# A mixture-of-experts layer on one core: tokens 1024 to 2047 routed through their eight experts alone, sorted by expert with indirect transfers

## What is computed

```
probs = sigmoid(x @ router_w.T + expert_bias)          # x: 2048 x 128, 160 experts
top_w, top_idx = top_k(probs, 8)
top_w = top_w / (sum(top_w) + 1e-9) * 2.5
combine = zeros(T, 160); combine[t, top_idx[t]] = top_w[t]
h1 = silu(einsum('th,eih->eti', x, w_gate))            # 64 inner columns an expert
routed = einsum('eti,ehi->th', h1 * combine.T[:, :, None], w_down)
shared = silu(x @ w_gate_shared.T) @ w_down_shared.T
out = x1 + gate_b * (routed + shared)
```

## Time and profile before

| what | us |
|---|---|
| median of three runs | 525.28 (525.02 to 528.24) |
| the profiled execution, whole | 521.39 |
| its span, from the first to the last instruction | 519.6 |
| PE busy | 495.6 (95%) |
| DVE busy | 431.3 (83%) |
| ACT busy | 392.2 (75%) |
| POOL busy | 150.6 (29%) |

### The profile page before, as it was taken

How to read it: one execution, slowest core, us unless ns; L and a number is a source line. 1 busy time by engine, 2 the same in 40 slices (tenths; PEclk the granted TensorE clock), 3 DMA queues, 4 the chain that set the end, 5 groups by cost and what they waited for, 6 DMA issues and landing times.

```text
span 519.6 us, 7819 instructions
## 1 busy us (share of the span) xinstructions
PE 495.6 (95%) x2159; PEld 396.0 (76%) x2159; DVE 431.3 (83%) x513; ACT 392.2 (75%) x440; POOL 150.6 (29%) x144
## 2 busy tenths in 40 slices
PE   7686699999999999999999999999999999999996
PEld 5475488777787788888888788788888888888885
DVE  5999888787878788787888797887878888788886
ACT  3267687787878787888888787878878787878873
POOL 3787434222222222222222222222222222222210
PEclk9699899999999999999999999999999999999999
DMA  7000899999999999999999999999999999999962
GB/s 240 1 1 8 216 226 265 227 225 226 234 227 233 242 236 240 230 235 239 230 239 231 221 241 233 232 245 234 237 236 239 242 239 244 233 239 231 225 176 81
DMA packets 38934, 110.15 MB, mean 212 GB/s; under 512 B 6564, under 2 KB 10788, under 8 KB 38920
## 3 DMA queue, kind: packets, MB, share of 16 engines
q1 hardware_dynamic: 38596, 109.32, 88.5%
q10 hardware_dynamic: 324, 0.67, 0.4%
HBM read 107.58 MB, written 2.38 MB: 212 GB/s over the span
## 4 chain that ended last, share of the span: by engine, by line
PE 74%; DMA 13%; DVE 8%; SPq 2%; issue 1%; ACT 1%; POOL 0%; DVEq 0%
PE ps L921 37%; PE ps L906 37%; DMA cb<-combine_scratch 10%; DVE gu L722 2%; DMA combine_scratch<-combT_b 1%; DMA x_sb<-x 1%; DVE stT L686 1%; SPq L280 1%; DVE picked L715 1%; DVE bn L600 1%; DVE picked L703 0%; PE ps L860 0%; DVE mod_gate L659 0%; DVE xn L615 0%; DVE top L698 0%
## 5 line engine op out<-in xcount | busy, mean ns | idle before, releaser
L722 DVE TENSOR_TENSOR gu<-ps,cb 128x1024 f32<-128x1024 f32 x161 | 196.7, 1222 | 76.8 <-DMA cb<-combine_scratch 69.3
L509 ACT ACTIVATE ps<-ps 128x1024 f32<-128x1024 f32 x161 | 162.1, 1008 | 62.8 <-PE ps L906 60.1
L729 DVE TENSOR_TENSOR g_lo<-gu,g_hi 128x1024 fp32r<-128x1024 f32 x162 | 199.8, 1233 | 0.1
L522 ACT ACTIVATE g_hi<-gu 128x1024 fp32r<-128x1024 f32 x162 | 170.9, 1055 | 29.2 <-DVE gu L722 24.7
L404 POOL TENSOR_TENSOR w_lo<-w_raw,w_hi 128x384 fp32r<-128x384 f32 x98 | 99.7, 1017 | 312.1 <-DVE g_lo L729 312.1
L906 PE MATMUL ps<-h_hi,w_hi 128*128 128x512 f32 x324 | 103.8, 401 | 4.1 <-DVE gu L722 1.7
L906 PE MATMUL ps<-h_hi,w_lo 128*128 128x512 f32 x324 | 102.1, 396 | 0.0
L906 PE MATMUL ps<-h_lo,w_hi 128*128 128x512 f32 x324 | 102.1, 396 | 0.0
L921 PE MATMUL ps<-g_lo,w_hi 128*128 128x512 f32 x324 | 100.6, 392 | 1.5 <-DVE g_lo L729 1.5
L921 PE MATMUL ps<-g_hi,w_hi 128*128 128x512 f32 x324 | 101.1, 393 | 0.0
L921 PE MATMUL ps<-g_hi,w_lo 128*128 128x512 f32 x324 | 101.0, 392 | 0.0
(11 more groups left out here) (99 smaller groups left out, 206.9 us busy)
## 6 DMA issues: line engine op xcount, KB each, us to landing
cb<-combine_scratch SPq DMA_DIRECT2D x322, 256.0 KB, 5.1
w_raw<-experts SPq DMA_DIRECT2D x54, 384.0 KB, 7.0
x_sb<-x SPq DMA_DIRECT2D x4, 256.0 KB, 4.9
out<-xn SPq DMA_DIRECT2D x3, 256.0 KB, 2.2
combine_scratch<-combT_a ACTq DMA_DIRECT2D x1, 512.0 KB, 5.5
wmod_sb<-wmod SPq DMA_DIRECT2D x1, 384.0 KB, 3.5
combine_scratch<-combT_a SPq DMA_DIRECT2D x1, 384.0 KB, 3.1
proj_sb<-proj SPq DMA_DIRECT2D x1, 272.0 KB, 4.9
```

Source lines behind the costliest of these rows:

```text
L509: act.activation(slot(z), slot(z), ACT.Silu).then_inc(silu_done, 1)
L522: act.activation(g_hi[:, k % RING, :], gu[:, k % RING, :], ACT.Copy).then_inc(hi_ready, 1)
L722: dve.tensor_tensor(gu[:, k % RING, :].rearrange("p (b n) -> p b n", b=2), slot(z), cb[:, k % RING, :].rearrange("p (b n) -> p b n", b=2), ...
L729: dve.tensor_tensor(g_lo[:, k % RING, :], gu[:, k % RING, :], g_hi[:, k % RING, :].bitcast(F32), ALU.subtract).then_inc(lo_ready, 1)
```

## The change

Tokens 0 to 1023 keep the dense way: 81 pair steps. They are cut in two pieces: pairs 0 to 44 (`DRAIN_TURN = 4`), and pairs 45 to 80 after the middle stage. For tokens 1024 to 2047 the following is new.

1. **Ranks (in the prologue).** DVE marks the chosen experts (`mark`), PE counts them with eight matmuls of 160 columns and ranks each token among those of its expert with 60 more (`count`, `rank`), DVE makes offsets and, for each token, the eight rows of the sorted order that it goes to (`place`, `row_idx`). `select`, `combine_weights` and `turn_combine` of these tokens go.
2. **Send (beside pairs 0 to 44).** POOL issues 64 indirect transfers (8 tiles x 8 choices), each of which scatters 128 rows of 512 bytes from `xn` to `x_rows` in DRAM: 6 and 6, then 5 behind each `weights_lo`.
3. **Middle stage, dense work stands still.** The shared expert for these tokens (2 block groups); 16 loads of 256 KB of sorted rows, turned on PE, kept by ACT and DVE (`load_sorted`, `turn_x`, `keep_x`); then 56 block groups of four blocks of 128 rows: 40 groups with the first 128 slots of each of the 160 experts, and 16 with 64 extra blocks for experts that have more, whose expert is read from a table at run time. A group is four plain float32 matmuls 64x128 (`block_inner`), one `silu` of ACT, four float32 matmuls 128x128 (`block_down`) and four copies of DVE that wait for each other (`keep_y`), with places read from memory into registers (`TENSOR_LOAD`) on PE and on DVE. Last, 16 banks are turned back and stored (`turn_y`, `keep_turned`, `y_rows`).
4. **Fetch (beside pairs 45 to 80).** POOL issues 64 indirect gathers from `y_rows`: from the third `weights_lo` on, 6 ahead of each, and 16 at the end. DVE adds each with its weight (`add_back`): 32 between the pairs, 32 after the last pair.

```diff
+ST = TILES - DT
+SLOTS = ST * P * TOPK
+BLK = 4
+FULL = NE // BLK
+EXTRA = 64
+XIN, WSR, WOV = 4, 2, 8
...
+            def load_full_weights(group):
+                slot = group % WSR
+                if group >= WSR:
+                    free = (WG * 2 * (group - WSR + 1) - 1 - SHARED) // BLK
+                    sp.wait_ge(yg_done, SH_GROUPS + free + 1)
+                sp.dma_start(ws_g[:, slot, :], experts[group, :, 0:WG * P]).then_inc(ws_loaded[slot], 16)
+                for a in range(2):
+                    sp.dma_start(ws_d[:, slot, a, :], experts[group, a * INTER:(a + 1) * INTER, WG * P:2 * WG * P]
+                                 ).then_inc(ws_loaded[slot], 16)
...
+            def load_extra_gates(first, end):
+                for o in range(first, end, BLK):
+                    if o >= WOV:
+                        sp.wait_ge(yg_done, extra_group(o - WOV) + 1)
+                    _, at = nc.values_load_multi_w_load_instructions(
                        tab_i[1:2, o:o + BLK], engines=(SP_ENGINE,), min_val=0,
                        max_val=WGROUPS * P * 12 - 12 * P + 11, skip_runtime_bounds_check_because=BOUNDED)
+                    for b in range(BLK):
+                        sp.dma_start(w_extra((o + b) % WOV)[0], gate_rows[bass.ds(at[b], P, 12), :]
+                                     ).then_inc(wov_gate[(o + b) % WOV], 16)
...
+            def block_inner(n):
...
+                if n >= 2:
+                    pe.wait_ge(g_done, n - 1)
...
+                for b in range(BLK):
...
+                        pr, a = full_expert(m, b)
+                        if b == 0 or pr % WG == 0 and a == 0:
+                            pe.wait_ge(ws_loaded[pr // WG % WSR], 48 * (pr // WG // WSR + 1))
...
+            for n in range(SH_GROUPS, ZGROUPS):
+                if n + 1 < ZGROUPS:
+                    block_inner(n + 1)
+                if n + 1 == TABLE:
+                    turn_table()
+                block_down(n)
...
+            for i in range(1, DRAIN_TURN + 1):
+                for s in range(BODY // WG):
+                    weights_lo(WG * i + s + 2, (s + 2) % RING)
+                    more = min(sent + 5, ST * TOPK)
+                    send(sent, more)
+                    sent = more
...
+            for n in range(back, ST * TOPK):
+                add_back(n)
```

More of the change, by code:

```diff
@@ L73 @@
 assert PAIRS == TURNS * BODY and WGROUPS * WG == PAIRS
+assert A_GU + RING * CHUNK == 2 * COLS
+PE_ENGINE, DVE_ENGINE = mybir.EngineType.PE, mybir.EngineType.DVE
+SP_ENGINE, POOL_ENGINE = mybir.EngineType.SP, mybir.EngineType.Pool
+BOUNDED = "the table is computed from counts that sum to the number of slots"
 def adaln_layer(nc: bass.Bass, x: bass.AP, columns: bass.AP, log_dt: bass.AP, rows: bass.AP,
@@ L305, in turn @@
                         sp.wait_ge(w_split, group + 1)
[L306 to L308 removed]
+                        load_weights(group + RING, k // WG)
+                    if not ((last or drain) and k + RING >= BODY):
                         sp.wait_ge(gated, j + 1)
                         load_combine(j + RING, k % RING)
[L312 to L318, removed]
@@ L770, in _, with pair @@
-            for c in range(CHUNKS):
-                if c > 0:
-                    turn(c, 0, False)
-                with dve.Fori(1, TURNS - 1) as i:
-                    turn(c, i, False)
-                turn(c, TURNS - 1, True)
+                    pair(i, k, (last or drain) and k == BODY - 1)
+            def pair(i, k, stop):
+                j = BODY * i + k
+                if not stop:
+                    ahead = k + 1
+                    use = BODY // RING * i + ahead // RING + 1
+                    dve.wait_ge(cb_loaded[ahead % RING], 32 * (use - (ahead % RING == 0)))
+                    gate(j + 1, ahead % RING, ahead)
+                gated_lo(j, k)
@@ new lines, in _ @@
+            first = BODY * (DRAIN_TURN + 1)
+            dve.wait_ge(cb_loaded[0], 32 * (first // RING))
+            gate(first, 0, 0)
+            back = 0
+            for i in range(DRAIN_TURN + 1, TURNS):
+                for k in range(BODY):
+                    pair(i, k, i == TURNS - 1 and k == BODY - 1)
+                    at = BODY * (i - DRAIN_TURN - 1) + k - 16
+                    if at >= 0 and at % 5 < 4:
+                        add_back(back)
+                        add_back(back + 1)
+                        back += 2
+                        if back == TOPK * GT:
+                            finish_sparse(0)
@@ L1016, in _, with turn @@
-            for c in range(1, CHUNKS):
-                turn_ffn(c, c)
+                    pe.wait_ge(w_split, WG * i + ahead // WG + 1)
+                inner(ahead % RING, ahead)
+            def turn(i, last, drain):
+                for k in range(BODY):
+                    next_inner(i, k, last or drain)
+                    down(BODY * i + k, k, last and k == BODY - 1)
+            with pe.Fori(1, DRAIN_TURN) as i:
+                turn(i, False, False)
+            turn(DRAIN_TURN, False, True)
```

809 lines of the change are left out of this document (642 added, 167 removed).

## The result

| | before | after |
|---|---|---|
| median (range) | 525.15 us (524.75 to 528.24, 4 runs) | 758.71 us (757.64 to 760.62, 4 runs) |
| span of the profiled execution | 519.6 us | 756.6 us |

The changed kernel takes 1.443 times as long (95% interval 1.437 to 1.450). The forecast was 688 us in a range of 590 to 790: right in sign and inside the range, 71 us too low.

A forecast was written before the change was run, and what follows sets the result against it. The prediction took PE and the DMA transfers to be both full. Its terms, 205 + 23 + 305 + 20 + 112 + 17, gave a span of 682 us and a median of about 688, in a range of 590 to 790 us.

The forecast's parts named there:

- pair 44 ends: End of the first dense part: 189 us, plus 4 for routing and 12 for the send, 205 us.
- 56 block groups: Middle stage: 332 us at half clock, 249 at full; two thirds at half clock taken, 305 us (212 to 355).
- turning back, restart: After the block groups: transposes 14 us, then 6 for the first `cb` transfer, 20 us (14 to 28).
- pairs 45 to 80 with the fetch: Second dense part: DVE, DMA and POOL just above 2.78 us a pair; 3.1 taken, 112 us (102 to 135).
- tail: After the last pair: the earlier 5.3 us and 12 more on DVE, 17 us (12 to 22).
- The waits for the weights: Full block groups: each of 25 later weight loads is waited for in full, 3.5 us each (2.5 to 4.5).
- The clock: Middle stage: PE's pauses of 3.5 us in every 4 to 7 put two thirds of it at half clock.
- The rival that the clock stays up: Middle stage all at full clock: 632 us in total; chance 0.20.
- The register load: Extra block groups: reading places from memory into registers takes 0.8 us (0.05 to 2.7).
- Send: Beside pairs 0 to 44: 64 indirect transfers cost 12 us of DMA traffic (0 to 18); POOL's 1.1 us issues hidden.
- The routing: `mark` to `place` on DVE, less the operations that go: +4 us (0 to 8).
- POOL the bound: Rival in both dense parts: 2.5 us an indirect transfer, +56 and +54 us, 798 us in total; chance 0.19.

The follow-up runs named there:

- e1: Four weight slots of six experts in place of two, against the changed kernel: span 672.2 us.
- e5: e1 with gate products widened to 128 weight columns (five of six) and down products contracting over 128 rows, in the full groups: span 612.4 us.
- e10: e5 with only the gate products widened; down products contract over 64 rows again: span 687.2 us.
- e11: e5 with only the down products widened to 128 rows; gate products take 64 weight columns again: span 616.3 us.
- e6: Changed kernel with four weight slots, twelve extra slots and three zero products of 512 columns behind each group: span 590.9 us.
- e4: Changed kernel with 52 of the 64 indirect sends replaced by plain SP transfers of the same size, so sorted rows are wrong: span 743.9 us.
- e3: Changed kernel with all but the first 12 sends issued behind the last `w_lo` of the first dense part: span 806.4 us.
- e9: Changed kernel with four weight slots, twelve extra slots, 48 extra blocks, array-filling products, no filler, and sorted-result stores spread between combine loads: span 549.8 us.
- e2: Changed kernel, still two weight slots, with six zero matmuls of 512 columns behind each `down` group: span 720.9 us.

## Why the prediction was right, and where it was off

The stages, by the borders shown above:

| term | forecast | measured |
|---|---|---|
| pair 44 ends | 205 | 224 |
| shared expert, sorted rows | 23 | 24 |
| 56 block groups | 305 | 341 |
| turning back, restart | 20 | 10 |
| pairs 45 to 80 with the fetch | 112 | 138 |
| tail | 17 | 20 |
| span | 682 | 757 |

The terms that came out too low add up to 85 us, and the turning back gives 10 of them back.

**The waits for the weights**: right in number (25) and place, 3.1 us each against 3.5. A third and fourth slot took off 81 us of what looked like 77.9. Shown by e1.

**The clock**: I counted two thirds of the middle at half clock. It was all of it but some 3 us at 252; my own half-clock sum of 332 us was nearer to the 341 than the 305 that I took. The rest is 0.48 us a matmul where the earlier trace rows had 0.42. The reason given, pauses as in the earlier trace rows, was the wrong one: it would have sent the reader to the slots, and with the slots mended the clock stayed. With the loads in time, what decided, by e5, e10 and e11, is that the down product uses 64 of the 128 rows; full products put beside it, as the filler of e6, raised the clock too. How the chip weighs them is not shown. The Trainium skill (TensorE: Matmul & The Clock Gate, section Part 1: The HAM clock gate (the "warmup" mystery)) ties the clock to how busy the PE has been; in e1 a PE that the profile calls busy for 100 of 100 us was not enough.

The rival that the clock stays up had an argument that was none. The earlier trace rows gives 1.00 for the first 13 us of the kernel before, but the matmuls there took as long as at half clock. Two of 512 columns at 10.80, at 14.57 (clock 1.00) and at 23.89 (clock 0.50):

```profile
10.80 2.05 PE L847 MATMUL ps<-hT,proj_sb 128*128 128x512 f32 x2 [1.02 <-ACT hT L445]
...
14.57 1.12 PE L847 MATMUL ps<-hT,proj_sb 128*128 128x512 f32 x2 [0.87 <-ACT hT L445]
...
23.89 2.08 PE L847 MATMUL ps<-hT,proj_sb 128*128 128x512 f32 x2 [0.87 <-ACT hT L445]
```

Why the row of clocks says 1.00 there is open; the length of a known matmul told more here.

**Turning back**, 10 us in place of 20: I took 14 for 64 transposes at half clock. They took 9.05, since the clock came up behind the block groups (0.93 in 592:598), and the 6 us for the first `cb` transfer were not paid at all: the restart at 598.84 waited 0.83 us, for ACT. That this offset brought the sum nearer to the measured time is luck.

**The register load**: I took 0.8 us. It was 0.30 to 0.34 (the TENSOR_LOAD rows of PE, DVE and SP). With four issues of 0.47 and a landing of 2.0, the period of the extra groups came out at 6.7 against 6.8; two errors in opposite directions, since the matmuls were slower.

**Send**: the sum, 12 us forecast and 17 measured, hides that the two prices were the wrong way round. Traffic, taken as 12 us, cost some 5 (e4); POOL's time, taken as nothing at 1.1 us an issue, cost some 12, because an issue is 1.26 at best and 1.8 to 2.0 where it meets a `g_lo`, with 1.26 just what I had found to be hidden.

**The routing**, `mark` to `place`, was taken as 4 us (bounds 0 and 8), and this is the largest miss of a bound in the first part: without the sends it still ended 14 us later than my 193. The timelines of PE place it. The first pair starts at 44.8 us before and at 45.3 in the changed kernel; the seventh starts at 71.08 before, at 88.67 in the changed kernel and at 87.64 in e3:

```profile
71.08 0.71 PE L906 MATMUL ps<-h_hi,w_hi 128*128 128x512 f32 x2
```

```profile
88.67 1.05 PE L1418 MATMUL ps<-h_hi,w_hi 128*128 128x512 f32 x2
```

So 17 us are lost by the seventh pair, and 18 at the end of the part in e3, whose later pairs run at 2.79 us: the loss lies among the first six pairs, where PE waits for DVE's `mask` (2.0 us) and `off_r` (2.7), counts and ranks. How much each step costs was not tried.

**POOL the bound**, the rival, was partly true, at about 1.5 us an issue instead of 2.5: three pairs take 10 to 12 us in both dense parts, not 8.34, and the second part runs at 3.8 us a pair where 3.1 was forecast. PE waiting for `w_lo` was one of the signs by which the forecast would be wrong, and it was seen (26.6 us). In the second part that gives 26 us over the forecast: 12.5 us of PE's waits for `w_lo`, 12.4 for `g_lo` (one of 9.0 behind the stores), and matmuls at a lower clock at places (0.82 in 604:632). I had used the Trainium skill (SBUF — State Buffer, section Who interferes with whom) to hold that `tensor_tensor` does not disturb POOL, and had read only its words on two-port modes. The same section of the Trainium skill also says that a DVE instruction with two inputs in SBUF contends with a GpSimd instruction that reads SBUF. The `g_lo` of 3.64 us agrees. That an indirect issue is held up by `g_lo` too is what the rows at 212.29 and 214.53 show; no run took `g_lo` away.

**Tail**: 3 us, of which 1.4 because the adding operations took 0.376 us one after the other, not 0.33: 12.02 us for 32 instead of 10.6.

```profile
738.93 12.02 DVE L1230 SCALAR_TENSOR_TENSOR xn<-arena,coef_s,xn 128x128 f32<-128x128 f32 x32
```

**Faster at all?** The 225 us of dense pairs are won, and no version here keeps more than they cost. The best, e9, took 551.5 us in one execution beside 523.5. Of its span 136 us are the middle (243.57 to 379.68), 22 the shared expert and the sorted rows, 8 the turning back, 14 the longer tail, together 180 of the 225. The two dense parts take 75 us more than their 81 pairs did before: 32.5 in the first (221.5 against 189), some 17 of them the routing, and 42.5 in the second (142.5 for 36 pairs in place of 100), while POOL issues 116 indirect transfers. Those 75 are the next to attack; how, was not tried.

## What to carry to other kernels

Before replacing dense work by chosen work, look at the shape of what remains: small products are paid by instruction and by clock, not by arithmetic, and with a contraction over 64 of 128 rows in half of the products the stage ran at half clock here until zeros filled the other half. A load that is issued when its slot comes free and needed by the next instruction is waited for in full: count slots by the order of the consumer, and look again at the clock when the wait is gone. An indirect transfer is POOL's time, 1.26 to 2.3 us each with its gap; if POOL also feeds the critical engine, that was the larger price here, not the bytes. And look at what an added instruction pushes its neighbours under: here `w_lo` came to lie under `g_lo`. Work of setting up that is woven into the first turns of the loop, as the routing here, costs more than its operations add up to: 17 us here, where 4 had been counted.

## What was not expected of the hardware

- A granted clock of 0.50 with PE busy for 100 of 100 us (e1), 0.50 with half of the products over 64 rows (e10), 0.97 when they contract over 128, half of it zeros (e5, e11). At one clock the width cost little: eight records of `down` took 1.16 us in e2 over 64 rows and in e11 over 128, and 1.06 in e5, where the gate before them was wide too.
- POOL's `w_lo` holds up DVE's two-operand `g_lo` (3.64 us in place of 1.22) and is not held up itself (1.05 us at most); `g_lo` holds up an indirect issue (1.94 us in place of 0.96) and is not held up by one (1.26 at most). The product that reads PSUM never took over 1.23.
- A plain transfer issued by POOL took it 0.52 us, an indirect one 0.96.
